# Distance attention: maxima subtracted one head at a time, and contexts divided and added from PSUM

## What is computed

```python
q, k, v = (h @ W.T + b).reshape(B, S, 16, 8)      # h = layernorm(x)
scores = einsum('bqhd,bkhd->bhqk', q, k) / sqrt(8)
pos_emb = dist_emb[255 + distance]                # out-of-range rows as the indexing clips them
scores += einsum('bqhd,qkd->bhqk', q, pos_emb) + einsum('bkhd,qkd->bhqk', k, pos_emb)
x = x + einsum('bhqk,bkhd->bqhd', softmax(scores), v)
```

## Time and profile before

| | us |
|---|---|
| median of the runs (4137.15, 10128.04, 4140.59) | 4140.59 |
| the profiled execution | 4119.65 |
| its span, first to last instruction | 4117.9 |
| distance attention within the span | 2590 to 3780 |
| busy: PE, DVE, ACT, POOL (whole span) | 3405.4, 3435.6, 2880.4, 1135.8 |

### The profile page before, as it was taken

One profiled execution on the slowest core, in us unless ns is written; L12 is line 12 of the kernel. 1 busy time (PEld: TensorE's weight loads), 2 busy tenths in 40 slices (PEclk: granted clock), 3 DMA queues, 4 the chain that ended last, 5 costly groups with the idle time before them and its releaser, 6 DMA issues. The chain is left out here.

```text
span 4117.9 us, 71243 instructions
## 1 busy us (share of the span) xinstructions
PE 3405.4 (83%) x27092; PEld 2091.6 (51%) x27092; DVE 3435.6 (83%) x4264; ACT 2880.4 (70%) x2433; POOL 1135.8 (28%) x983
## 2 busy tenths in 40 slices
PE   3899999999999999999947943788888898897990
PEld 2333333333333333333335941687887887887790
DVE  7999999999999999999937545688788787887762
ACT  3999999999999999999803413565666665664530
POOL 2112121122122221112100542534334325330235
PEclk8999999999999999999977976899999999997995
DMA  5000000000000000000032224412213112112122
GB/s 157 7 13 6 13 13 12 7 13 13 6 13 13 6 13 13 6 13 13 5 107 68 65 53 164 65 25 39 40 18 48 31 25 44 28 18 74 27 64 67
DMA packets 237592, 146.43 MB, mean 36 GB/s; under 512 B 147104, under 2 KB 220416, under 8 KB 236832
## 3 DMA queue, kind: packets, MB, share of 16 engines
q1 hardware_dynamic: 228640, 125.03, 12.7%
q0 software_dynamic: 8704, 17.84, 1.8%
HBM read 90.73 MB, written 52.10 MB: 35 GB/s over the span
## 5 line engine op out<-in xcount | busy, mean ns | idle before, releaser
L698 PE MATMUL psA<-wave,diag 128*128 128x512 f32 x3072 | 1441.4, 621 | 137.1 <-DVE score L854 89.3
L766 ACT ACTIVATE wave<-wave 128x2048 f32<-128x2048 int32 x640 | 1181.2, 1904 | 3.6 <-DVE wave L841 2.2
L698 PEld LDWEIGHTS psA<-wave,diag 128*128 128x128 f32 x3072 | 582.8, 196 | 896.2 <-issue 699.8
L635 POOL TENSOR_TENSOR diag<-ident,par 128x128 f32<-128x128 f32 x384 | 291.3, 784 | 1423.8 <-PE psA L698 1423.8
L816 DVE TENSOR_SCALAR wave<-s,par 128x2048 int32<-128x2048 int32 x480 | 617.3, 1286 | 0.0
L841 DVE TENSOR_SCALAR wave<-wave 128x2048 int32<-128x2048 int32 x512 | 613.4, 1227 | 0.0
L1730 POOL COPY kb<-ks 48x1024 bf16<-48x1024 bf16 x160 | 331.1, 2069 | 587.9 <-PE psR L1790 404.0
L1871 ACT COPY r<-psR 128x1024 f32<-128x1024 f32 x320 | 310.7, 1025 | 152.1 <-PE psR L1790 152.1
L1880 ACT ACTIVATE W<-psR 128x1024 f32<-128x1024 f32 x256 | 253.2, 1024 | 167.4 <-PE psR L1815 164.7
L731 ACT ACTIVATE s<-psS,par 128x1024 int32<-128x1024 f32 x256 | 282.8, 1105 | 121.8 <-PE psS L661 121.8
L854 DVE SCALAR_TENSOR_TENSOR score<-wave,par,psA 128x1024 f32<-128x1024 f32 x256 | 318.9, 1281 | 37.0 <-PE psA L698 37.0
(11 more groups left out here) (259 smaller groups left out, 4469.3 us busy)
## 6 DMA issues: line engine op xcount, KB each, us to landing
ks<-kb_parts SPq DMA_DIRECT2D x56, 384.0 KB, 6.2
qs<-qb_parts SPq DMA_DIRECT2D x32, 384.0 KB, 6.3
ys<-f_ys SPq DMA_DIRECT2D x36, 256.0 KB, 2.5
wave_out<-og SPq DMA_DIRECT2D x33, 256.0 KB, 2.1
o<-wave_out SPq DMA_DIRECT2D x8, 1024.0 KB, 5.3
qp<-qa_parts SPq DMA_DIRECT2D x32, 192.0 KB, 3.4
kp<-ka_parts SPq DMA_DIRECT2D x32, 192.0 KB, 3.9
f_wu<-in_w_up SPq DMA_DIRECT2D x2, 2048.0 KB, 11.0
```

Source lines behind the costliest of these rows:

```text
L635: ins = pool.tensor_tensor(diag[:, h % 2, f, :], ident[:], par[:, u, 1, h * NF + f:h * NF + f + 1] .to_broadcast((P, P)), ALU.mult)
L698: mm = pe.matmul(psA[:, kt, :], diag[:, h % 2, f, :], wave[:, h % 2, f, kt * L:(kt + 1) * L], start=(f == 0), stop=(f == PE_F - 1), skip_g ...
L766: act.activation(wave[:, h % 2, f, :], angle[:, h % 2, f, :], ACT.Sin, scale=float(TWO_PI / 2.0 ** 32)).then_inc(sine, 1)
```

## The change

`subtract` becomes two tensor_scalar instructions, one per head, with the head's maximum as a scalar per partition; `shifted` now counts heads. `turn` waits for each head ahead of its four matmuls, and takes its slot before the first wait. In `context` the product with the reciprocal is written back in place into the PSUM slot, the tile `ctxt` is gone, the sum with X reads the slot, and `dve_took` is raised by the sum instead of the product.

```diff
-        ctxt = sb(c, "ctxt", [P, H, HD])
...
             def turn(q, j):
-                pe.wait_ge(shifted, q * NPAIR + j + 1)
                 slot = free_slot(fill["e", q, j])
                 for i in range(2):
+                    pe.wait_ge(shifted, q * BH + 2 * j + i + 1)
                     for kt in range(QT):
...
             def subtract(q, j):
-                hs = slice(2 * j, 2 * j + 2)
                 dve.wait_ge(m_ready, 4 * q + j // 4 + 1)
-                dve.tensor_tensor(S[:, hs, :], S[:, hs, :],
-                                  m[:, hs].rearrange("p (h a) -> p h a", a=1).to_broadcast((P, 2, L)),
-                                  ALU.subtract).then_inc(shifted, 1)
+                for h in (2 * j, 2 * j + 1):
+                    dve.tensor_scalar(S[:, h, :], S[:, h, :], m[:, h:h + 1], None, ALU.subtract).then_inc(shifted, 1)
...
             def context(q, i):
...
-                dve.tensor_tensor(ctxt[:], out[:, :, 0:HD],
+                dve.tensor_tensor(out[:, :, 0:HD], out[:, :, 0:HD],
                                   rec[:].rearrange("p (h a) -> p h a", a=1).to_broadcast((P, H, HD)),
-                                  ALU.mult).then_inc(dve_took, 1)
-                dve.wait_ge(dve_took, by_dve["o", q, i])
-                dve.tensor_tensor(X[:, b * QT + qt, :], X[:, b * QT + qt, :],
-                                  ctxt[:].rearrange("p h d -> p (h d)"), ALU.add).then_inc(ctx_step, 1)
+                                  ALU.mult).then_inc(ctx_step, 1)
+                dve.wait_ge(ctx_step, at + 2)
+                dve.tensor_tensor(X[:, b * QT + qt, :].rearrange("p (h d) -> p h d", d=HD),
+                                  X[:, b * QT + qt, :].rearrange("p (h d) -> p h d", d=HD), out[:, :, 0:HD],
+                                  ALU.add).then_inc(dve_took, 1)
```

## The result

The changed kernel takes 4109.51 us (median of 6 runs, 4101.54 to 4118.69) against 4145.54 for the kernel before on the same occasions. The ratio is 0.9918 with a 95% interval of [0.9904, 0.9933], so 28 to 40 us less. One of the six runs of the kernel before took 10128.04 and is left out of the ratio.

What follows compares the result with a forecast made beforehand. PE was taken to set the pace, waiting 49.5 us for DVE's subtraction. -28.6 (usual passes) + 3.3 (POOL passes) + 9.9 (contexts) + 4 (clock) = -11.4 us, from median 4140.59 to 4129; range 4102 to 4156, own range 4117 to 4141.

Steps and rivals of the forecast that it cites:

- the rival in which the contexts are hidden: Context slots: later release hidden from PE and no fall of the clock, 14 us less, 4115; chance 0.12.
- Rate of the subtraction: New DVE subtraction: 498 ns per head, a pair 0.83 us against 1.13, 0.30 less.
- The rival with one element per cycle: DVE subtraction: heads of 751 ns, a pair 1.33 us against 1.13, total 4138; chance 0.12.
- What reaches PE in a usual pass: 13 of 16 passes: e5 starts 2.2 us earlier on PE, 28.6 us off.
- Three passes with POOL's copies: Subtractions beside POOL's copies: a held head costs a copy plus its own time, PE loses 1.1 us each, 3.3 on.
- Contexts: Context slots: released 0.33 us later by the sum, at 30 waits of PE, 9.9 us on.
- Clock: PE between turned units: two more of 15 stretches fall below a granted clock of 1.00, 4 us on.
- Waits of PE: Turns: mid-turn waits cost nothing where both heads are there; PE's wait for subtractions falls from 49.5 us to under 20.
- the slower rival: Turns on PE: the wait between heads stops PE 0.22 us in each of 256 turns, 4185; chance 0.08.
- Median against the profiled execution: Whole kernel: the sum gives 4108.3 from the profiled 4119.65, but 4129.2 from the runs' median of 4140.59.

Runs made afterwards that it cites:

- s0: Not a run: DVE's first subtraction of a pass, for a pair of heads; one instruction before, two in the changed kernel.
- e0: Not a run: PE's first turn of a pass, turning a pair of heads after their subtraction; the turned unit is counted from its first matmul.
- second profile of before: The kernel before, unchanged, profiled once more: 1131.3 us from the first turned unit to the last, against 1127.6 in its first profile.
- The tensor_tensor of 683 ns: The changed kernel, each head subtracted by a 128x512 tensor_tensor with the maximum broadcast instead of a tensor_scalar: 4144.87 us, ratio 1.0009 to the kernel before.
- s5: Not a run: DVE's subtraction of the pair of heads that e5 turns; in the fourth pass it ends 18.9 us after s0 began, 19.2 before.
- e5: Not a run: PE's turn of the pair that s5 subtracts; in the fourth pass it takes 1.97 us before and 1.04 in the changed kernel.
- e6: Not a run: PE's turn that follows e5; from e5 to e6 the three passes with POOL's copies took 16.1 us before and 9.9 after.
- the contexts alone: The kernel before with only the new contexts (product in PSUM, slot freed by the sum), subtraction unchanged: 4146.50 us, ratio 1.0006.
- the later release: The kernel before, ctxt kept in SBUF, only that the sum with X instead of the product frees the slot: 4169.86 us, ratio 1.0064.
- The late spread: The changed kernel, POOL's second four copies in three passes waiting until all 32 heads are subtracted: 4093.95 us, ratio 0.9887 to the kernel before.
- the old contexts: The changed kernel with the contexts put back (ctxt in SBUF, slot freed by the product): 4099.16 us, ratio 0.9894 to the kernel before.
- the pair wait: The changed kernel, a turn waiting for both heads of its pair ahead of its first matmul: 4120.56 us, ratio 0.9946 to the kernel before.
- the subtraction by heads alone: The changed kernel's subtraction by heads, contexts as in the kernel before: 4099.16 us, ratio 0.9894 to the kernel before.

## Why the prediction was right, and where its sum was off

The time lay in the range and moved as forecast. The sum, -11.4, came out as -29 to -33 in the stage's own time. That it still lay in the range is in part luck: 4109.51 is below the forecast's own 4117 to 4141 and near the 4115 of the rival in which the contexts are hidden, and they are not. By its steps:

- **Rate of the subtraction**: right. 480 ns against 498, and each head 0.396 after the last (4 in 1.67) against 0.415. The rival with one element per cycle is out; it needed 751. The Trainium skill's formula ("VectorE: DVE Perf Modes", The TRN2 errata) gave an estimate of 327, and the measurement decides against that too: by 480 ns for 512 elements and 1286 for 2048 the fixed part is about 210 ns, an estimate, where its 58 cycles are 60. The same section says itself that this row is too low and puts the measured fixed part at about 150 cycles.
- **What reaches PE in a usual pass**: right. Forecast 2.2. Counted from the start of s0 to the start of the pass's last turning matmul, a usual pass went from 28.95 to 26.64, 2.3 less (1.95 in the turned unit, and e0 0.35 sooner). Twelve of them make 27.7; the last pass, with no next one to prepare, won 3.6 (3.1 against the second profile of before).
- **Three passes with POOL's copies**: the term that failed. Forecast 3.3 on, by "a head costs a copy plus its own time". A held head costs the copy alone, 2.07: the eight copies follow each other in 16.52, so the head runs without delaying the next one, which a 1.22 us tensor_tensor did (20.53). The tensor_tensor of 683 ns lies between: there the eight copies took 18.11, and a held head 2.40, about what was forecast. s5 ends 18.9 after s0 instead of 20.8, and e5 starts 0.54 sooner than before, where 1.1 later was forecast: 1.6 off in the three passes. Counted as above, though, they went from 39.27, 39.86 and 39.89 to 37.06 to 37.08, 7.8 off in all and 11 us from the forecast. The other 6.2 is PE's clock from e5 to e6 (16.1 to 9.9, above), for which the sum had no term: its clock is that of the stretches between turned units alone. It was not one execution's chance. In all 15 such units of the five profiles with pairs (before and the contexts alone twice each, the later release) e5 took 1.97; in all 21 of the seven with tensor_scalar heads it took 1.04. The late spread shows what the hold of four copies is worth, 15.6 us more. Of the Trainium skill's rule ("SBUF — State Buffer", Who interferes with whom) the trace agrees with one side, that the DVE instruction waits out the GpSimd one; the other side, that GpSimd waits as long in turn, no copy here shows behind a head of 480 ns.
- **Contexts**: right. 0.33 per release, 0.66 in a pass, 43.07 against 42.42 with the old contexts. That the old contexts take 10 us off by the medians, as the sum had it (9.9), is partly chance: in the stage it is 16.5 and 17.7, of which the release is 9.9 and the rest the clock's.
- **Clock**: wrong in its sign. Two more stretches below 1.00 were taken for 4 us; there were nine at 1.00 instead of six or seven, so fewer below it. From one pass's last turn to the next s0 the fifteen stretches sum to 643.7 us, against 634.1 before (638.4 in its second profile): 5.3 to 9.6 more, where the contexts alone make 15 x 0.67 = 10. The clock gave back 0 to 5 there, besides the 6.2 within the three turned units.

-27.7 - 3.6 - 7.8 + 9.6 = -29.5 is the stage's change against the first profile, within 0.3 of what the turns show; the forecast had -28.6 + 3.3 + 13.9.

- **Waits of PE**: in the middle of a turn right; the slower rival (45 ns per turn to decide) is out by the pair wait. The wait for subtractions was to fall under 20 and fell to 27.1, because PE still waits 20.8 in the three passes with POOL's copies.
- **Median against the profiled execution**: setting the difference on the median of the runs was right, since the profiled execution of before was 28 us short outside of the stage. The 4108.3 worked out from that execution lies 1 us from the measured time, but by luck: too low a start and too small a gain cancel.

What stays open: why the contexts alone cost 10 us on top of the subtraction by heads and only 2.5 on top of the kernel before. The release costs the same 0.66 per pass in both. Over the fifteen stretches, summed as above, the contexts cost 17.4 in the one case (626.3 to 643.7), and in the other 4.0 more or 0.3 less than before (638.1). The stretches at full clock went from 14 to 9 in the one and from 6 or 7 to 11 in the other, which has the right sign. What in the order of the waits decides which stretch falls was not tried.

## What to carry to other kernels

Price a faster instruction by how long the engine behind it still waits for it, here 2.3 us in a usual pass although DVE became 83 us less busy in this line. When a buffer's last reader is split in two, free it by the first step if that copies the data out: what is saved in SBUF is paid at every refill of a full ring. And look at which instructions of another engine hold this one: moving twelve copies of POOL out of its way was worth 15.6 us, nearly half of what the change brought.

## What the runs showed of the hardware that was not expected

- A tensor_scalar of 480 ns between two POOL copies is held for up to the whole of a copy (21 heads of 512 took over 1 us, at most 2.17) but does not delay the next one: eight copies in 16.52 us, where eight without a subtraction beside them took 16.39 (the late spread). A tensor_tensor of 683 ns did delay them, to 18.11, and one of 1219 ns to 20.53.
- Three kernels profiled twice had the same count of stretches at full clock both times, and the length of a stage of 1100 us within 1.2; the kernel before did not (6 and 7, 3.7 us). Two kernels that differ by 0.33 us at 30 waits differ by 5 stretches of 15.
- In the passes with POOL's copies PE ran at a granted 0.54 to 0.69 from e5 to e6 in every unit with pairs and at 1.00 in every one with tensor_scalar heads, 4.72 to 5.79 us against 3.30 for the same work.
- A sum of 128x128 with one input in PSUM took 286 to 288 ns in all 32 cases, 12 of them beside a POOL copy. Its form with two SBUF inputs took as much as 2079 beside such copies (the subtraction by heads alone).
